# The last layer's head of a four-layer graph network: copies of turned points reordered, sign rows on GpSimd, distances over 128 rows

## The reference

```python
deg = jnp.maximum(adj.sum(axis=1, keepdims=True), 1e-08)
w = adj / deg
log_ij = _logmap(x[:, None, :], x[None, :, :], c)   # for all 4096 x 4096 pairs
agg = jnp.einsum('ij,ijc->ic', w, log_ij)
transformed = agg @ weight + bias
return _expmap(origin, transformed, c)
```

## Time and profile before

| | |
|---|---|
| median of 3 runs | 1671.05 us (1670.82 to 1675.09) |
| profiled execution, its own time | 1681.84 us |
| its span | 1679.8 us |
| mean granted TensorE clock | 0.95 |
| busy PE, DVE, ACT, POOL | 1525.2, 1169.5, 948.8, 295.1 us |
| last periods of the third layer up to the first distances | about 1027 to 1157 us |
| the 80 units | about 1157 to 1625 us |
| closing part | about 1625 to 1680 us |

### The profile page before, as it was taken

How to read it: one execution, slowest core, us unless ns; L and a number is a source line. 1 busy time by engine, 2 the same in 40 slices (tenths; PEclk the granted TensorE clock), 3 DMA queues, 4 the chain that set the end, 5 groups by cost and what they waited for, 6 DMA issues and landing times.

```text
span 1679.8 us, 20794 instructions
## 1 busy us (share of the span) xinstructions
PE 1525.2 (91%) x7945; PEld 641.9 (38%) x7990; DVE 1169.5 (70%) x1579; ACT 948.8 (56%) x920; POOL 295.1 (18%) x150
## 2 busy tenths in 40 slices
PE   5999999989999699999999999899789989989870
PEld 1433334333333444444454444444233333333330
DVE  4677755557887555756848747466868787887867
ACT  1243488853434333333334345757879898998954
POOL 1000000000000000000000014484345343444430
PEclk9999999999999599999999999999789999999995
DMA  9999679969998234442433431246134454444400
GB/s 338 412 413 413 276 303 409 409 244 383 412 413 330 113 151 158 177 167 102 176 124 151 151 114 63 77 142 233 50 126 158 150 182 136 162 140 150 160 17 25
DMA packets 118106, 348.95 MB, mean 208 GB/s; under 512 B 6324, under 2 KB 31224, under 8 KB 117752
## 3 DMA queue, kind: packets, MB, share of 16 engines
q1 hardware_dynamic: 106784, 329.27, 52.2%
q10 hardware_dynamic: 11224, 18.36, 2.9%
HBM read 329.78 MB, written 17.83 MB: 207 GB/s over the span
## 4 chain that ended last, share of the span: by engine, by line
PE 58%; issue 17%; POOL 11%; DVE 7%; DMA 4%; ACT 2%; SPq 1%; POOLq 0%; DVEq 0%; ACTq 0%
PE ps L751 17%; PE ps L878 13%; POOL ring L651 11%; PE ps L884 10%; DMA ring<-in_adjT 4%; PE ps L690 3%; PE ps L689 3%; PE ps L823 2%; PE ps L907 2%; PE ps L715 1%; PE ps L705 1%; PE ps L771 1%; PE ps L913 1%; DVE work L1652 1%; DVE work L1639 1%
## 5 line engine op out<-in xcount | busy, mean ns | idle before, releaser
L878 PE MATMUL ps<-ring,X 128*64 128x512 f32 x512 | 264.1, 597 | 13.3 <-DVE ring L1900 13.3
L1156 ACT ACTIVATE work<-ps,code_bias 128x1024 uint8<-128x1024 f32 x128 | 135.8, 1111 | 247.4 <-PE ps L690 238.7
L879 PE MATMUL ps<-work,X 128*64 128x512 f32 x512 | 264.1, 598 | 0.0
L631 POOL TENSOR_SCALAR work<-ring 128x1024 int16<-128x1024 uint8 x24 | 70.2, 2932 | 1033.8 <-DMA ring<-codes 981.8
L1287 ACT ACTIVATE work<-ring 128x2048 f32<-128x2048 f32 x64 | 122.2, 1912 | 216.8 <-PE ps L886 195.8
L651 POOL TENSOR_TENSOR ring<-ring,work 128x1024 f32<-128x1024 f32 x80 | 189.7, 2371 | 273.5 <-DVE work L2156 273.3
L884 PE MATMUL ps<-work 128*64 128x512 bf16 x768 | 208.4, 380 | 0.0
L886 PE MATMUL ps<-work 128*64 128x512 bf16 x768 | 208.4, 380 | 0.0
L977 PE MATMUL ps<-work 96*128 96x512 f32 x320 | 168.8, 652 | 0.0
L751 PE MATMUL ps<-ring,work 128*64 128x512 f32 x704 | 160.8, 598 | 1.6 <-DMA ring<-in_adjT 1.6
L1897 DVE TENSOR_SCALAR work<-ring 128x2048 bf16<-128x2048 f32 x64 | 78.5, 1227 | 106.9 <-PE ps L886 106.7
(11 more groups left out here) (324 smaller groups left out, 2660.7 us busy)
## 6 DMA issues: line engine op xcount, KB each, us to landing
ring<-in_adjT SPq DMA_DIRECT2D x90, 2048.0 KB, 11.2
work<-in_adjT SPq DMA_DIRECT2D x26, 2048.0 KB, 15.3
ring<-in_adjT SPq DMA_DIRECT2D x48, 1024.0 KB, 7.9
codes<-work ACTq DMA_DIRECT2D x64, 256.0 KB, 6.1
ring<-codes SPq DMA_DIRECT2D x32, 512.0 KB, 3.7
ring<-in_adjT SPq DMA_DIRECT2D x32, 512.0 KB, 3.5
X<-in_x ACTq DMA_DIRECT2D x1, 1024.0 KB, 7.0
work<-in_xT SPq DMA_DIRECT2D x2, 512.0 KB, 23.6
```

What stands on the lines that cost most here:

```text
L878: nc.tensor.matmul(ps[0:F, h, :], rows, ring[:, r, k, cols], start=start, stop=stop)
L879: nc.tensor.matmul(ps[F:P, h, :], rows, negs[:, pair, i, cols], start=start, stop=stop)
L1156: nc.scalar.activation(codes[:, u, k:k + 2, :].rearrange("p k c -> p (k c)"), ps[:, bank:bank + 2, :].rearrange("p k c -> p (k c)"), ACT.Relu,
```

## The change

**Order of the copies.** In `copy_nodes` ACT now goes first: it makes `UT` as soon as the points are turned, DVE copies its rows after that, and ACT makes the tail (`copy_tails`) and the sign rows (`copy_signs`) one tile later, or, for quarter 2, at the end of the same period. Quarter 2 is copied at n = 0 instead of 1. `copy_last_nodes` is turned round in the same way. `gather(0)` no longer waits for sign rows.

**Sign rows.** Those of quarter 2 are made by POOL (`copy_third_signs`, two instructions of 3 x 1024) after unit 2. All sign rows move to other places: partitions 96 to 98 of `VT`, and of two rooms of weights that are no longer used.

**128 rows.** `UT` and `VT` now span all 128 partitions in `distances`. POOL sets partitions 96 to 127 of both to zero (two memsets of 32 x 4096 f32) after its decay tile 14; the sign rows in `VT` meet zeros of `UT`.

**Odd jobs.** `move_x(0)` goes from n = 3 to 6 and its copy from 4 to 7; `make_points(1)` from n = 4 to 1; `centre_rows` from 2 to 3, `row_spread` from 3 to 4, and `root2(2)` from 4 to 5.

```diff
-        dist_region = carve(N)
-        UT = dist_region[0:ROWS, :]
-        signs_w = dist_region[MOVE:MOVE + 3, 0:N // 2].bitcast(BF16)
-        signs_m = dist_region[MOVE:MOVE + 3, N // 2:N].bitcast(BF16)
-        VT = carve(N)[0:ROWS, :]
+        UT, VT = carve(N), carve(N)
+        sign_rows = slice(MOVE, MOVE + 3)
+        signs_w, signs_m = (
+            [low[:, 0:QC], low[:, QC:2 * QC], high[:, 0:QC], high[:, QC:2 * QC]]
+            for low, high in ((VT[sign_rows, 0:QC].bitcast(BF16), mid_w[sign_rows, :].bitcast(BF16)),
+                              (VT[sign_rows, QC:2 * QC].bitcast(BF16), early_w[sign_rows, :].bitcast(BF16))))
...
-        MOVED_AT = [3] + [u.n + 3 for u in own_units if u.last and u.I < NQ - 1]
+        MOVED_AT = [6] + [u.n + 3 for u in own_units if u.last and u.I < NQ - 1]
         LAST_AT = 8
-        POINTS_AT = [4, 14, 32]
+        POINTS_AT = [1, 14, 32]
...
+                if i == 14:
+                    pool.wait_ge(normed[1], NQ)
+                    pool.wait_ge(support_ready, NQ)
+                    pool.wait_ge(decay_pool, i + 1)
+                    nc.gpsimd.memset(UT[ROWS:P, :], 0.0).then_inc(rows_cleared, 1)
+                    pool.wait_ge(rows_cleared, 1)
+                    nc.gpsimd.memset(VT[ROWS:P, :], 0.0).then_inc(rows_cleared, 1)
+                    pool.wait_ge(rows_cleared, 2)
+
+            def copy_third_signs():
+
+                cols = slice(2 * QC, 3 * QC)
+                pool.wait_ge(ut_copied, 3)
+                nc.gpsimd.tensor_scalar(signs_w[2], UT[F:F + 3, cols], -FAR / DIST_SCALE, None,
+                                        ALU.mult).then_inc(signs_copied, 1)
+                pool.wait_ge(vt_tail_copied, 3)
+                pool.wait_ge(signs_copied, 5)
+                nc.gpsimd.tensor_copy(signs_m[2], VT[F:F + 3, cols]).then_inc(signs_copied, 1)
+                pool.wait_ge(signs_copied, 6)
...
+                if u.n == 2:
+                    pool.wait_ge(weighted, u.n + 1)
+                    copy_third_signs()
...
+                if u.n == 0:
+                    pe.wait_ge(rows_cleared, 2)
+                    pe.wait_ge(signs_copied, 4)
...
-                    pe.wait_ge(signs_copied, 6)
...
             def copy_nodes(n):
 
-                act.wait_ge(vt_copied, n + 1)
+                act.wait_ge(uv_ready, n + 1)
...
+            def copy_tails(n):
...
+            def copy_signs(n):
+
+                act.wait_ge(rows_cleared, 2)
...
+                if i in OUT_AT:
+                    copy_nodes(OUT_AT.index(i))
                 if i - 1 in OUT_AT:
-                    copy_nodes(OUT_AT.index(i - 1))
+                    copy_tails(OUT_AT.index(i - 1))
+                    copy_signs(OUT_AT.index(i - 1))
...
-                act.wait_ge(vt_copied, 4 + h)
+                act.wait_ge(uv_ready, 4 + h)
...
+                if n == 0:
+                    copy_nodes(2)
                 if unit_at(n + 1):
                     raise_dist(units[n + 1])
+                if n == 5:
+                    root2(2)
                 if u:
                     nc.scalar.activation(u.log, u.log, ACT.Exp, scale=-0.5).then_inc(inv_made, 1)
                 if n == 0:
                     copy_sums2(NQ - 1)
-                if n == 1:
-                    copy_nodes(2)
-                if n == 4:
-                    root2(2)
+                    copy_tails(2)
...
             def copy_nodes(n):
 
-                dve.wait_ge(uv_ready, n + 1)
+                dve.wait_ge(ut_copied, n + 1)
...
+                if n == 0:
+                    copy_nodes(2)
                 if unit_at(n + 1):
                     multiply(units[n + 1])
...
-                if n == 1:
-                    copy_nodes(2)
                 if n == 2:
                     read_sums2(NQ - 1)
                 if n == 3:
+                    centre_rows(2, NQ - 1)
+                if n == 4:
                     row_spread(2, NQ - 1)
```

More of the change, by code:

```diff
@@ L85, in adjacency_stack @@
         code_bias = sb("code_bias", [P, 1])
[L86 to L89, removed]
+        early_w = sb("early_w", [P, 16 * F])
+        cheb_sb = early_w[:, 0:4 * F].rearrange("p (k o) -> p k o", o=F)
+        turn_w = early_w[:, 4 * F:10 * F].rearrange("p (i o) -> p i o", i=3)
+        w_edge = early_w[:, 10 * F:13 * F]
+        w_att = early_w[:, 13 * F:16 * F]
+        mid_w = sb("mid_w", [P, 16 * F])
+        w_hid = mid_w[0:F + 1, 0:8 * F].rearrange("p (g n) -> p g n", g=2)
+        winT_sb = mid_w[0:F, 8 * F:11 * F]
+        gatWT_sb = mid_w[0:F, 11 * F:13 * F]
+        w_first = mid_w[0:F, 13 * F:14 * F]
+        later_or_self = mid_w[:, 14 * F:15 * F].bitcast(BF16)
+        minus_ones = mid_w[:, 15 * F:16 * F].bitcast(BF16)
         w_score = sb("w_score", [P, 2])
-        w_hid = sb("w_hid", [F + 1, 2, 4 * F])
-        w_att = sb("w_att", [P, 3 * F])
-        gatWT_sb = sb("gatWT_sb", [F, 2 * F])
         gat_a_sb = sb("gat_a_sb", [F, 2])
-        winT_sb = sb("winT_sb", [F, 3 * F])
         w2_sb = sb("w2_sb", [P, 2 * F])
@@ L387, in adjacency_stack @@
         last_signs_copied = sem("last_signs_copied")
+        rows_cleared = sem("rows_cleared")
         dist_ready = sem("dist_ready")
@@ L637, in copy_last_signs @@
                 pool.wait_ge(ut_copied, 4 + h)
-                nc.gpsimd.tensor_scalar(signs_w[:, cols], UT[F:F + 3, cols], -FAR / DIST_SCALE, None,
+                nc.gpsimd.tensor_scalar(signs_w[3][:, h * HALF:(h + 1) * HALF], UT[F:F + 3, cols], -FAR / DIST_SCALE, None,
                                         ALU.mult).then_inc(last_signs_copied, 1)
@@ L989, in push_apart @@
                     cols = slice(u.I * QC + h * HALF, u.I * QC + (h + 1) * HALF)
-                    mm = nc.tensor.matmul(ps[:, u.banks + h, :], signs_w[:, u.rows * P:(u.rows + 1) * P],
-                                          signs_m[:, cols], start=False, stop=True, skip_group_check=True)
+                    mm = nc.tensor.matmul(ps[:, u.banks + h, :], signs_w[u.J][:, u.k * P:(u.k + 1) * P],
+                                          signs_m[u.I][:, h * HALF:(h + 1) * HALF], start=False, stop=True, skip_group_check=True)
                 mm.then_inc(far_added, 1)
@@ L1334, in copy_nodes @@
             def copy_nodes(n):
-                act.wait_ge(vt_copied, n + 1)
+                act.wait_ge(uv_ready, n + 1)
                 cols = slice(n * QC, (n + 1) * QC)
                 banks = ps[:, 2 * n:2 * n + 2, :].rearrange("p h c -> p (h c)")
-                nc.scalar.activation(UT[:, cols], banks[0:ROWS], ACT.Copy, scale=-2.0 * DIST_SCALE).then_inc(
+                nc.scalar.activation(UT[0:ROWS, cols], banks[0:ROWS], ACT.Copy, scale=-2.0 * DIST_SCALE).then_inc(
                     ut_copied, 1)
+            def copy_tails(n):
+                cols = slice(n * QC, (n + 1) * QC)
+                banks = ps[:, 2 * n:2 * n + 2, :].rearrange("p h c -> p (h c)")
                 nc.scalar.activation(VT[F:ROWS, cols], banks[MOVE:U_COLS], ACT.Copy).then_inc(vt_tail_copied, 1)
-                nc.scalar.activation(signs_w[:, cols], banks[F:F + 3], ACT.Copy, scale=2.0 * FAR).then_inc(
+            def copy_signs(n):
+                act.wait_ge(rows_cleared, 2)
+                cols = slice(n * QC, (n + 1) * QC)
+                banks = ps[:, 2 * n:2 * n + 2, :].rearrange("p h c -> p (h c)")
+                nc.scalar.activation(signs_w[n], banks[F:F + 3], ACT.Copy, scale=2.0 * FAR).then_inc(
                     signs_copied, 1)
-                nc.scalar.activation(signs_m[:, cols], banks[MOVE:MOVE + 3], ACT.Copy).then_inc(signs_copied, 1)
+                nc.scalar.activation(signs_m[n], banks[MOVE:MOVE + 3], ACT.Copy).then_inc(signs_copied, 1)
             copy_sums(3)
@@ L2024, in read_sums2 @@
                                 ALU.add).then_inc(bias_added, 1)
-                centre_rows(2, Q)
             copy_sums(3)
@@ L2056, in _ @@
                     read_sums2(READ_AT.index(i))
+                    centre_rows(2, READ_AT.index(i))
                 if i in SPREAD_AT:
```

8 lines of the change are left out of this document (3 added, 5 removed).

## The result

The changed kernel takes 1659.99 us (median of 20 runs, 1651.99 to 1671.00) against 1672.46 us for the kernel before in as many runs; the ratio is 0.9927, with a 95% interval of 0.9908 to 0.9947. On the 1671.05 us that were shown that is 1658.9 us: 12 us faster, where 16 were forecast, and within the range. The profiled execution's span is 1662.8 us, 17.0 less than before's 1679.8. Both profiles are of executions longer than these medians, by 4.9 and 9.4 us, so 4.5 of the 17.0 us are scatter and not the change. All ratios are of fast executions; one of the kernel before, 2388.75 us at a mean clock of 0.61 in the call of the last four runs, is left out.

The account below looks back on a forecast made before the run. PE and ACT were taken as nearly level in the 80 units, slowed by early waits and some 55 us at low clock. Terms -4.6, -1.2, -1.9, 0, 0, -0.6, -8 sum to -16.3 us: 1655 us, range 1643 to 1669.

Parts of the forecast that it names:

- Copies of quarter 2: Main term, before unit 1: ACT without four copies in a row reaches its Ln sooner; 4.6 us gain, bounds 3.3 and 4.9.
- Odd jobs: First periods of the units: no period has two odd jobs, ACT's wait behind move_x goes; 1.2 us gain, bounds 0 and 2.4.
- Last quarter: Periods 9 and 11: ACT copies first, without two 0.94 us waits for DVE; 1.9 us gain, bounds 0 and 1.9.
- Sign rows on POOL: After unit 2: 5.7 us together on POOL, unit 3 some 2 us late; effect taken 0, bounds 0 and +2 us.
- Memsets: POOL at about 1088 to 1095 us: two take 6.7 us; effect taken 0, up to +2.4 us if DVE is held.
- Third layer: Its last tiles: two node copies made sooner, so tile 27 comes 0.6 us sooner; bound above no gain.
- The clock: Distances in the units: 128 rows may mean fewer and shorter low-clock stretches; 8 us gain, bounds 0 and 20.
- Rival 1: Distances in the units: the clock does not react to the rows; -8.3 us, 1663 us; chance 0.27.
- rival 2: First units: the start's gain is given back through POOL's queue, memsets holding DVE and late distances; 1670 us, chance 0.13.
- Rival 3: PE in every unit: 128 rows expose weight loads, up to 15 us in all; slower, +7, 1678 us; chance 0.07.

Follow-up runs that it names:

- doubled run: Changed kernel with both memsets made twice, four in a row on POOL after its tile 14: 1671.31 us, ratio 0.9978 to the kernel before.
- v_split: Changed kernel with each move_x cut in two halves in successive periods (the cut version): 1654.11 us, ratio 0.9869 to the kernel before.
- v_split96: Changed kernel with each move_x cut in two and the distances over 96 rows: 1659.83 us, ratio 0.9914 to the kernel before.

## Why the prediction was right, and where not

- **Copies of quarter 2.** Right in mechanism and size: 4.6 us forecast, 4.0 between the two profiles in the first three steps, 5.2 to 6.4 when it is undone, and the lower bound named what comes next, the distances of unit 3 at a low clock, for which ACT waits 1.77 us.
- **Odd jobs.** Wrong by the size: 1.2 forecast, nothing measured, at the bound of 0. Behind `move_x` at period 6 ACT waits only 0.62 us for the distances (at 1208.22 of its timeline), not 2.36, but with the odd jobs back units 0 to 14 take no longer.
- **Last quarter.** Mis-sized: 1.9 forecast, with 1.9 as the bound too; 5.1 us in its two steps when undone, because a late copy makes PE idle and the clock fall. The clock's reaction belongs to the price of a wait. In the time it can't be resolved. By the steps this term is as large as the one called main: undoing either makes units 0 to 14 take 89.3 us.
- **Sign rows on POOL.** Right that the time doesn't show them. But their path was another: not POOL's queue, in which they took 2.76 and 1.51 us (1.03 in four other profiles) and not 5.7 together, but DVE, of which they cost 1.6 us in one profile of the changed kernel and 0.3 in the other.
- **Memsets.** Right: hidden; 7.8 us where 6.7 were worked out. They held DVE for 6 us, more than the 3.3 that the prediction feared, in a stretch where DVE had idle time. The doubled run shows that POOL had little to spare.
- **Third layer.** Right by the number, though the row gives "issue" as what ended the wait, and not ACT: PE's wait of 1.61 us before tile 27 is 1.10 in the profile after, 0.5 us of the 0.6. In all profiles with the new order that step is 4.0 us, in all with the old one 4.5.
- **The clock.** Right that the rows matter, wrong by its size: this is the term that was mis-sized. "I take a third of that, 8 us" stands against 2 to 4 us between 96 and 128 rows in the new order, and 5 in the old. The low clock in the units did fall by 41 us, but the order alone takes away 24 of them, and their gain is in the other terms' steps.
- **The sum.** -16.3 on the profiled execution, where the two profiles differ by 17.0; 16 on the median, where 12 were measured. That the sum came so near is in part luck: the clock term was 4 to 6 us too much and the odd jobs 1.2, while the last quarter was 3.2 too little and the first copies 0.6 or more.

Rival 1 was wrong in its mechanism, but its time of 1663 lay as near as 1655, so the total alone doesn't decide between them. Of rival 2's mechanisms POOL's queue isn't there, and the hold on DVE is there and costs nothing that the time shows. Rival 3's would have shown at 0.10 us a unit; the spacing is unchanged.

What stays open: why the clock is low for 41 us in the layers before in one execution and for 65 in another, how the third layer's 0.5 us enters the total, and whether the rest of the 5.7 us between v_split and v_split96 is more than scatter.

## What to carry to other kernels

Where two engines are level and the clock falls after short idle times, the price of a wait is not its length: here two waits of about 1 us cost 5 together, as PE idled behind them and the clock fell after the first. Look first for waits and for clumps of small products, cut the clumps and fill the idle with them. Where single runs scatter more than the effect, measure from one repeated event to the next inside the profile and let the medians only confirm it.

## What the runs showed of the hardware

- With zeros in 32 more rows the same product takes the same time (592 ns a record, weight load 190 ns), but the clock was low for 17 and 20 us in the units instead of 34 with 96 rows (one profile), and for 7 to 14 (three profiles) instead of 20 (one) in the cut version.
- The clock fell after idle times of PE of only 1.0 to 2.3 us, and after 2.00 us of 64 x 64 products, but neither every time: it stayed full after one of two idle times of 2.25 us, and at 7 of 24 places of the products. Cut into two of 1.10 us, these were followed by full clock at all twelve later places of four profiles.
- While GpSimd made sign rows of 3 x 1024, a VectorE instruction of 128 x 8 took 1.02 us instead of 0.17, and one of 128 x 1024 1.94 instead of 1.22; during its two memsets four conversions of 128 x 1024 bytes took 8.8 us instead of some 2.8.
- A GpSimd memset of 32 x 4096 f32 took 3.85 to 3.94 us, 0.95 ns a column, a little above the 0.8 of small ones.
